# Shifts of three norms in a transformer block: minus the mean written by VectorE with one input, multiplied by the root on GpSimd behind the root

## The chip, the cores and the metric

The kernel runs on one core of one Trainium2 chip. Its time is the device time of one execution in microseconds (us), here the median of several runs. The profile is of one execution, and its span runs from the first to the last instruction.

The engines are TensorE (PE for its products, PEld for its weight loads), VectorE (DVE), ScalarE (ACT), GpSimd (POOL) and SyncE (SP), whose queue issues the DMAs. Each engine works through its own list in order and waits on semaphores for the others.

## What is computed

The input `x` has 8 x 2048 rows of 256 numbers. Everything is float32.

```python
x = L0_attn_x
xn = _layernorm(x)                     # first norm, no gain and offset
# inside s = _L0_attn_ref(xn, ...)
q, k, v = split(xn @ Wqkv + bqkv)
qp, kp = elu(q) + 1, elu(k) + 1
attn = (qp @ (kp^T v)) / (qp . sum(kp) + 1e-6)      # per batch of 2048 rows
z = layer_norm(xn + attn, g1, b1)      # second norm
ffn = (silu(z @ Wg + bg) * (z @ Wu + bu)) @ Wd + bd
s = layer_norm(z + ffn, g2, b2)        # third norm
g = silu(xn @ (ternary(weight) * scale)^T)
return x + s * g
```

A norm of a row is `row * root + shift`, with root = 1/sqrt(variance + eps) and shift = -mean * root. The change is about who computes these shifts.

## The kernel before

**Tiling.** The 16384 rows are cut into 32 groups of 512 rows (four tiles of 128), four groups to a batch. One loop over the groups is laid out as a pipeline: in the iteration that does the feed-forward net of group f, the attention of group f+1, the norm and the turned copy of group f+6 and the last norm of group f-1 are done as well. In front of it stands a filling phase, behind it two iterations that drain it. Each product is done as three products of split (high and low) parts, and the low parts are subtractions on VectorE.

**Order.** What each engine does in an iteration, and in which order, is a list written by hand: `TENSOR_JOBS`, `SCALAR_STEPS`, `VECTOR_STEPS`, `GPSIMD_STEPS`, with `FILL_...`, `END_...` and `DRAIN_...` for the ends. An engine that waits in one step holds up all steps behind it.

**The three norms.** Number k is 0 for the first norm, 1 for the one behind attention, 2 for the last. For each, VectorE takes the statistics of four tiles (`stats`, L922) and aggregates them into `mv` (`aggregate`, L929, mean and variance), and writes variance + eps into `ve` (L933). GpSimd raises it to -0.5 (`rstd`, L569). Then VectorE writes the shift from mean and root with one operation on [128, 4]: `nmr0` in `a_norm` (L978), `nmr1` in `attn_norm` (L1064), `nmr2` in `last_shift` (L1131). ScalarE applies root and shift to the rows: `x_norm` (first four groups only) and `x_res` for norm 0, `z_rows` for norm 1, `last_rows` for norm 2. From the fifth group on, `a_norm` also writes the normed rows itself (L974), from mean and root.

**Steps near the change.** On VectorE the iteration begins with `zT_low` (L1085), `k_add` (L1014) and `ffn_rows` (L1117), then `last_stats`, the four `attn` steps (L1048, L1051, L1054, L922) with `last_shift` between the first two, `h_rows` 0 (L1095), `k_max` 0 (L1021), `h_low` 0 (L1105), `h_rows` 1, `a_stats`, `h_low` 1, `q_aggregate`, `h_rows` 2, `a_norm`, `x_turn` (L985), `attn_norm`, and so on to `q_low` 1 (L1042) and `h_low` 5. On GpSimd it begins with `xn_low` 0 (L579), `last_rstd`, `last_gain` 0 (L602, waits for `last_rows` 0), `z_g1` 0 (L642), `last_offset` 0 (L608), `xn_low` 1 and `sum_k` 0 (L592, waits for `k_max` 0); later come `a_rstd` and `q_rstd`, the other row operations, `last_add` 3 (L621, releases the output's DMA and the next load of `xq` on SP's queue), and `tail_again` (L655), which waits for `h_rows` 5.

**Banks.** Products go round a ring of five PSUM banks. A job may start once the job five places before it has been read (`freed`). So product job Q 1 waits for `h_low` 1 of VectorE, the job U 0 for `attn` 0, and the job K 1 for `h_low` 3.

Of the kernel before, what the change touches and what calls it, by code (L numbers as in the profile page):

```python
# [31 lines left out]
D = 256  # L32
# [29 lines left out]
LN0 = LEAD + 1  # L62
# [21 lines left out]
def fill(text):  # L84
# [13 lines left out]
    h_high 3, x_high 1, h_high 4, silu_gate 5, xn_high 0, xn_high 1, h_high 5""")  # L98
VECTOR_STEPS = steps("""
    xk_low 0, zT_low 0, k_add 0, zT_low 1, kv_bias 0, kv_bias 1, kv_low 0, kv_low 1, ffn_rows 0,  # L100
    ffn_rows 1, k_add 1, last_stats 0, attn 0, last_shift 0, attn 1, attn 2, attn 3, h_rows 0, k_max 0,
    h_low 0, h_rows 1, a_stats 0, h_low 1, q_aggregate 0, h_rows 2, a_norm 0, x_turn 0, attn_norm 0,
    k_max 1, h_low 2, k_low 0, q_elu 0, z_turn 0, q_elu 1, q_low 0, k_low 1, h_rows 3, h_rows 4,
    q_low 1, h_low 3, x_low 0, h_rows 5, x_low 1, h_low 4, h_low 5""")
GPSIMD_STEPS = steps("""
# [10 lines left out]
    silu_gate 5, h_high 5, tail_last 0""")  # L116
END_VECTOR = steps("""
    zT_low 0, zT_low 1, ffn_rows 0, h_rows 0, ffn_rows 1, h_low 0, last_stats 0, h_rows 1, h_low 1,
    last_shift 0, h_rows 2, h_low 2, h_rows 3, h_rows 4, h_low 3, h_low 4, h_rows 5, h_low 5""")
END_GPSIMD = steps("""  # L120
    end_terms 0, z_g1 0, last_rstd 0, z_g1 1, z_g1 2, last_gain 0, last_offset 0, last_gain 1,
    last_gain 2, last_offset 1, last_gate 0, last_offset 2, last_add 0, last_gain 3, last_gate 1,
# [29 lines left out]
    k_add 3 1, a_stats 5 0, k_max 3 1, xT_low 4 0, setup_ternary 0 0, q_elu 1 0, xk_low 0 0, xT_low 4 1,  # L152
    k_add 4 0, kv_bias 0 0, kv_bias 0 1, a_norm 5 0, kv_low 0 0, kv_low 0 1, x_turn 5 0, k_max 4 0,
    k_add 4 1, attn 0 0, k_low 4 0, k_max 4 1, setup_ternary_parts 0 0, attn 0 1, attn 0 2, attn 0 3,
    q_aggregate 0 0, k_low 4 1, attn_norm 0 0, setup_d_tail 0 0, x_low 5 0, q_elu 1 1,
    setup_hidden_biases 0 0, x_low 5 1, q_low 1 0, q_low 1 1""")
FILL_GPSIMD = fill("""
    setup_masks 0 0, a_rstd 0 0, a_rstd 0 1, a_rstd 1 0, sum_k 0 0, sum_k 0 1, a_rstd 2 0, sum_k 0 2,
# [54 lines left out]
def build_kernel(nc, x, wqkv, bqkv, wg, bg, wu, bu, wd, bd, g1, b1, g2, b2, wt, out):  # L213
    f32, f32r = mybir.dt.float32, mybir.dt.float32r
    ALU, ACT = mybir.AluOpType, mybir.ActivationFunctionType
# [8 lines left out]
    with ctx:  # L224
# [3 lines left out]
        def sem(name):  # L228
# [20 lines left out]
        rstd0 = sb("rstd0", [P, LN0, TILES])  # L249
# [21 lines left out]
        nmr0 = sb("nmr0", [P, LN0, TILES])  # L271
        mv = sb("mv", [P, 3, TILES, 2])
# [8 lines left out]
        xn = sb("xn", [P, TILES, D])  # L281
        kp = sb("kp", [P, KP, 2, D])
# [10 lines left out]
        rstd1, nmr1 = norm1[:, 0, :], norm1[:, 1, :]  # L293
        rstd2, nmr2 = norm2[:, 0, :], norm2[:, 1, :]
# [32 lines left out]

        names = ("warm first_act first_warm w_bq1 w_bk w_qkh w_qkl w_abs w_sum w_scale w_half "
                 "w_vh w_vl w_neg w_tern w_ternT w_tern_r w_b1w w_row w_hb w_guh w_gul w_db w_dh w_dl w_dt "
                 "bn0 ag0 ve0 rs0 xn nm0 xh xl tn tz TX xTh xTl K k1 mK eK kp kph kpl ks XK xk xkl KV kv kvh kvl "  # L330
                 "Q mQ eQ qp qph qpl N d1 d2 xr r bn1 ag1 ve1 rs1 nm1 z TZ zTh zTl zg B sg "
                 "G GU S h hh hl ha D r2 bn2 ag2 ve2 rs2 nm2 n2 a b c o bs gs xb a_last o_last").split()
        S = {n: sem("s_" + n) for n in names}

        def parts3(hi_l, lo_l, hi_r, lo_r):

            return ((hi_l, hi_r), (lo_l, hi_r), (hi_l, lo_r))

        def job_bank(kind, g, n):
            return bank[NUMBER[kind, g, n] % RING]  # L340
# [199 lines left out]
        def _(eng):  # L540
# [140 lines left out]
            for i in ITERATIONS:  # L681
                a, q, f, last = i + LEAD, i + 1, i, i - 1
# [234 lines left out]
        def _(eng):  # L917
# [18 lines left out]
            def first_stats(p):
                pair = slice(2 * p, 2 * p + 2)
# [23 lines left out]
            def a_norm(g, p=0):  # L961
                if g == 0:
                    return first_norm(p)
                eng.wait_ge(S["rs0"], g + 2)
                if g == PLAIN:
                    eng.wait_ge(S["xn"], TILES * PLAIN)
                    eng.wait_ge(S["XK"], TILES * (g - 1))
                if g > PLAIN:
                    eng.wait_ge(S["xl"], PAIRS * (g - PLAIN))
                    eng.wait_ge(S["TX"], PAIRS * min(g, TURNED))  # L970
                if g > TURNED:
                    eng.wait_ge(S["tn"], g - TURNED)
                for t in range(TILES if g >= PLAIN else 0):
                    eng.tensor_scalar(normed(g)[:, t, :], xa[:, g % 2, t, :], mv[:, 0, t, 0:1],  # L974
                                      rstd0[:, g % LN0, t:t + 1], ALU.subtract, ALU.mult).then_inc(S["xn"], 1)
                if g >= LN0:
                    eng.wait_ge(S["xr"], TILES * (g - LN0 + 1))
                eng.scalar_tensor_tensor(out=nmr0[:, g % LN0, :], in0=mv[:, 0, :, 0], scalar=-1.0,  # L978
                                         in1=rstd0[:, g % LN0, :], op0=ALU.mult, op1=ALU.mult).then_inc(S["nm0"], 1)

            def x_turn(g, _=0):
                if g >= TURNED:
# [74 lines left out]
                eng.wait_ge(S["r"], n + 1)  # L1057
                stats(1, g, t, rz[:, g % RZ, t, :])

            def attn_norm(g, _=0):  # L1060
                eng.wait_ge(S["rs1"], g + 1)
                if g:
                    eng.wait_ge(S["z"], TILES * g)
                eng.scalar_tensor_tensor(out=nmr1, in0=mv[:, 1, :, 0], scalar=-1.0,  # L1064
                                         in1=rstd1, op0=ALU.mult, op1=ALU.mult).then_inc(S["nm1"], 1)

            def z_turn(g, _=0):
                if not ZT0 <= g < ZT1:
                    return
# [50 lines left out]
            def last_stats(g, _=0):  # L1120
# [13 lines left out]
            def end_rows(g, _=0):

# [113 lines left out]
            for i in ITERATIONS:  # L1249
# [230 lines left out]
```

## Time and profile before

| | |
|---|---|
| median of 3 runs | 1210.86 us (1210.26 to 1211.26) |
| profiled execution: its time | 1212.66 us |
| profiled execution: span | 1211.0 us |
| TensorE products busy | 1190.9 us, 98% |
| VectorE busy | 1082.2 us, 89% |
| ScalarE busy | 953.3 us, 79% |
| GpSimd busy | 841.7 us, 70% |
| granted TensorE clock | 0.998 of full speed |

The profiled execution took 1.66 us more than its span, which lies ahead of the first and behind the last instruction, and 1.8 us more than the median of the runs. Busy time of TensorE is modelled, since products are pipelined; whether it really waits is read from the distances between the starts of its products.

### The profile page before, as it was taken

The page shows a single profiled execution, that of the slowest core. Times are in us where ns is not written, and L with a number is a line of the kernel's source. Part 1 is how long each engine was busy: PE and PEld are TensorE (multiplying, and loading weights), DVE is VectorE, ACT ScalarE, POOL GpSimd, SP SyncE. Part 2 cuts the span into 40 slices and gives each one's busy share as a digit, 9 for nine tenths or more (in the row PEclk, how much of TensorE's full clock was granted, in tenths as well). Part 3 has the DMA queues.
Part 4 walks back from the last instruction along what each step waited for, and adds up shares of the span by engine and source line. Part 5 has one row for each costly group of instructions (what it writes and reads, how often), then busy time and mean ns, then how long its engine had stood idle before and what let it go on. Part 6 is the DMA issues. An engine that isn't in the chain of part 4 may idle for free.

```text
span 1211.0 us, 24021 instructions
## 1 busy us (share of the span) xinstructions
PE 1190.9 (98%) x7550; PEld 1070.2 (88%) x7550; DVE 1082.2 (89%) x2467; ACT 953.3 (79%) x1557; POOL 841.7 (70%) x994
## 2 busy tenths in 40 slices
PE   8999999999999999999999999999999999999997
PEld 6889998989988999989999988999988899888886
DVE  6988999999999999999999999999999999777765
ACT  7787888878888887888878888778797788867753
POOL 3443787767787776787767777667776677766676
PEclk9999999999999999999999999999999999999999
DMA  7213432334432334432234432234332343222201
GB/s 217 74 50 88 123 106 70 88 105 123 123 104 72 87 106 123 118 103 78 87 106 122 121 104 74 74 120 123 108 96 63 101 123 105 70 71 61 76 22 35
DMA packets 137524, 115.61 MB, mean 95 GB/s; under 512 B 12340, under 2 KB 122294, under 8 KB 137399
## 3 DMA queue, kind: packets, MB, share of 16 engines
q1 hardware_dynamic: 137398, 114.08, 32.2%
q8 instruction: 62, 1.02, 0.3%
q14 instruction: 64, 0.52, 0.1%
HBM read 67.38 MB, written 46.67 MB: 94 GB/s over the span
## 4 chain that ended last, share of the span: by engine, by line
PE 86%; DVE 7%; issue 2%; ACT 2%; DMA 1%; POOL 1%; SPq 0%; DVEq 0%; POOLq 0%; ACTq 0%
PE bank L1271 61%; PE d_bank L1271 17%; PE xk_bank L1271 7%; DVE st L922 1%; DMA z_turned<-xa 1%; DMA xa<-z_turned 1%; DVE rz L1054 1%; PE bank L1285 1%; DVE bank L1095 0%; DVE h_l L1105 0%; ACT rz L695 0%; DVE zT_l L1085 0%; POOL norm L569 0%; ACT hs L695 0%; DVE kp L1014 0%
## 5 line engine op out<-in xcount | busy, mean ns | idle before, releaser
L1271 PE MATMUL bank<-zT_h,wgu_h 128*128 128x512 f32 x704 | 275.6, 391 | 1.1 <-DVE rz L1054 1.0
L1271 PE MATMUL bank<-zT_l,wgu_h 128*128 128x512 f32 x704 | 275.7, 392 | 0.0
L1271 PE MATMUL bank<-zT_h,wgu_l 128*128 128x512 f32 x704 | 275.4, 391 | 0.0
L695 ACT ACTIVATE rz<-rz,norm 128x256 f32<-128x256 f32 x252 | 140.5, 596 | 57.7 <-DVE norm L1131 57.1
L569 POOL TENSOR_TENSOR norm<-ve,consts 128x4 f32<-128x4 f32 x64 | 72.9, 1139 | 153.6 <-DVE ve L933 153.5
L1271 PE MATMUL d_bank<-wd_h,h_h 128*128 128x256 f32 x640 | 179.2, 280 | 0.1
L1271 PE MATMUL d_bank<-wd_h,h_l 128*128 128x256 f32 x640 | 179.0, 280 | 0.0
L1271 PE MATMUL d_bank<-wd_l,h_h 128*128 128x256 f32 x640 | 179.0, 280 | 0.0
L1095 DVE SCALAR_TENSOR_TENSOR bank<-bank,hb,hs 128x512 f32<-128x512 f32 x160 | 117.9, 754 | 54.0 <-ACT hs L695 42.3
L695 ACT ACTIVATE h_h<-bank 128x512 fp32r<-128x512 f32 x160 | 95.8, 599 | 80.9 <-DVE bank L1095 80.5
L1271 PEld LDWEIGHTS bank<-zT_l,wgu_h 128*128 128x128 f32 x704 | 132.1, 188 | 28.8
L1271 PEld LDWEIGHTS bank<-zT_h,wgu_h 128*128 128x128 f32 x704 | 132.7, 189 | 25.8 <-DVE rz L1054 3.3
L695 ACT ACT_TABLE_LOAD x116 | 148.8, 1283 | 4.1 <-POOL wd_l L678 1.2
L1271 PEld LDWEIGHTS bank<-zT_h,wgu_l 128*128 128x128 f32 x704 | 132.2, 188 | 20.6
L695 ACT ACTIVATE hs<-bank,hb 128x512 f32<-128x512 f32 x192 | 128.3, 685 | 15.0 <-PE bank L1271 13.6
L592 POOL TENSOR_TENSOR ksum<-ksum,kp 128x256 f32<-128x256 f32 x120 | 106.9, 891 | 46.7 <-DVE kp L1021 43.3
L1105 DVE TENSOR_TENSOR h_l<-bank,h_h 128x512 fp32r<-128x512 f32 x160 | 110.0, 688 | 23.1 <-ACT h_h L695 17.4
L1271 PEld LDWEIGHTS d_bank<-wd_h,h_h 128*128 128x128 f32 x640 | 120.2, 188 | 3.1 <-DVE h_l L1105 0.5
L1271 PEld LDWEIGHTS d_bank<-wd_h,h_l 128*128 128x128 f32 x640 | 120.2, 188 | 2.7
L1271 PEld LDWEIGHTS d_bank<-wd_l,h_h 128*128 128x128 f32 x640 | 122.0, 191 | 0.0
L642 POOL TENSOR_TENSOR rz<-rz,g1b 128x256 f32<-128x256 f32 x128 | 118.0, 932 | 0.0
L602 POOL TENSOR_TENSOR rz<-rz,g2b 128x256 f32<-128x256 f32 x124 | 90.4, 739 | 35.0 <-ACT rz L695 35.0
(163 smaller groups left out, 3576.3 us busy)
## 6 DMA issues: line engine op xcount, KB each, us to landing
xq<-in_L_attn_x_dram SPq DMA_DIRECT2D x32, 512.0 KB, 6.0
xa<-in_L_attn_x_dram SPq DMA_DIRECT2D x31, 512.0 KB, 3.9
out_dram<-rz SPq DMA_DIRECT2D x31, 512.0 KB, 5.0
z_turned<-xa SPq DMA_DIRECT2D x120, 128.0 KB, 3.3
xa<-z_turned SPq DMA_DIRECT2D x30, 512.0 KB, 4.1
turned<-xa SPq DMA_DIRECT2D x108, 128.0 KB, 2.5
xa<-turned SPq DMA_DIRECT2D x27, 512.0 KB, 3.9
rz<-in_L_attn_Wg_dram SPq DMA_DIRECT2D x1, 640.0 KB, 5.2
```

The lines of the kernel that those rows point to most:

```text
L569: eng.tensor_tensor(dst, ve[:, k, :], neg_half[:, 0:1].to_broadcast([P, TILES]), ALU.pow).then_inc(S[f"rs{k}"], 1)
L592: eng.tensor_tensor(ksum[:, slot, :], ksum[:, slot, :], part, ALU.add).then_inc(S["ks"], 1)
L602: eng.tensor_tensor(row_, row_, g2b[:, :], ALU.mult).then_inc(S["a"], 1)
L642: eng.tensor_tensor(row_, row_, g1b[:, :], ALU.mult).then_inc(S["zg"], 1)
L695: return eng.activation(out_, in_, func, **kw).then_inc(S[name], 1)
L922: eng.bn_stats(st[:, k, t, :], rows).then_inc(S[f"bn{k}"], 1)
L1054: eng.scalar_tensor_tensor(out=rz[:, g % RZ, t, :], in0=num[:, 0:D], scalar=den[:, n % 2, 1:2], in1=rz[:, g % RZ, t, :], op0=ALU.mult, op1 ...
L1095: eng.scalar_tensor_tensor(out=hidden(g, c)[0:rows, :], in0=up, scalar=hb[0:rows, HC + c:HC + c + 1], in1=hs[0:rows, n % 2, :], op0=ALU.ad ...
L1105: eng.tensor_tensor(h_l[:, slot, :], hidden(g, c)[:, :], h_h[:, slot, :].bitcast(f32), ALU.subtract).then_inc(S["hl"], 1)
L1271: ins = eng.matmul(dst, left, right, start=first and n == 0, stop=last and n == len(pairs) - 1, **kw)
L1285: ins = eng.transpose(dst[:, c * D + t * P:c * D + (t + 1) * P], src[:, 2 * p + t, c * P:(c + 1) * P], ident[:, :])
```

## The change

The shift is now made in two parts. VectorE writes minus the mean into the place of the shift, straight behind `ve`, with an operation that has one input. GpSimd, straight behind the root, waits for both and multiplies that place by the root. The steps `attn_norm` and `last_shift` and the operation at the end of `a_norm` are gone from VectorE. New semaphores `ng0` to `ng2` count the minus means; `nm0` to `nm2` still count finished shifts, now signalled by GpSimd. The very first group keeps its own path (`first_stats`, `first_norm`). The last group of norm 2 needs no shift: VectorE still writes minus its mean, GpSimd leaves the multiply out.

```diff
 VECTOR_STEPS
-    ... last_stats 0, attn 0, last_shift 0, attn 1, ...
+    ... last_stats 0, attn 0, attn 1, ...
-    ... a_norm 0, x_turn 0, attn_norm 0, k_max 1, ...
+    ... a_norm 0, x_turn 0, k_max 1, ...
...
+        def shift_of(k, g):
+            return nmr0[:, g % LN0, :] if k == 0 else nmr1 if k == 1 else nmr2
...
 def rstd(k, g, dst):            # GpSimd
                 eng.tensor_tensor(dst, ve[:, k, :], neg_half[:, 0:1].to_broadcast([P, TILES]),
                                   ALU.pow).then_inc(S[f"rs{k}"], 1)
+                if k == 2 and g == GROUPS - 1:
+                    return
+                eng.wait_ge(S[f"rs{k}"], g + 1 + (k == 0))
+                eng.wait_ge(S[f"ng{k}"], g + (k > 0))
+                to = shift_of(k, g)
+                eng.tensor_tensor(to, to, dst, ALU.mult).then_inc(S[f"nm{k}"], 1)
...
 def aggregate(k, g):            # VectorE
-                    if g and t == 0:
-                        eng.wait_ge(S[f"nm{k}"], g + (k == 0))
+                    if g > (k == 0) and t == 0:
+                        eng.wait_ge(S[f"ng{k}"], g - (k == 0))
+                    if g == 1 and k == 0 and t == 0:
+                        eng.wait_ge(S["nm0"], 2)
...
                 eng.tensor_scalar(ve[:, k, :], mv[:, k, :, 1], LN_EPS, None, ALU.add)\
                    .then_inc(S[f"ve{k}"], 1)
+                if k == 0 and g >= LN0:
+                    eng.wait_ge(S["xr"], TILES * (g - LN0 + 1))
+                if k == 1 and g:
+                    eng.wait_ge(S["z"], TILES * g)
+                if k == 2 and g:
+                    eng.wait_ge(S["n2"], TILES * min(g, GROUPS - 1))
+                eng.tensor_scalar(shift_of(k, g), mv[:, k, :, 0], -1.0, None, ALU.mult).then_inc(S[f"ng{k}"], 1)
...
 def a_norm(g, p=0):             # VectorE
-                if g >= LN0:
-                    eng.wait_ge(S["xr"], TILES * (g - LN0 + 1))
-                eng.scalar_tensor_tensor(out=nmr0[:, g % LN0, :], in0=mv[:, 0, :, 0], scalar=-1.0,
-                                         in1=rstd0[:, g % LN0, :], op0=ALU.mult, op1=ALU.mult).then_inc(S["nm0"], 1)
...
-            def attn_norm(g, _=0):
-                eng.wait_ge(S["rs1"], g + 1)
-                if g:
-                    eng.wait_ge(S["z"], TILES * g)
-                eng.scalar_tensor_tensor(out=nmr1, in0=mv[:, 1, :, 0], scalar=-1.0,
-                                         in1=rstd1, op0=ALU.mult, op1=ALU.mult).then_inc(S["nm1"], 1)
...
-            def last_shift(g, _=0):
-                if g < GROUPS - 1:
-                    eng.wait_ge(S["rs2"], g + 1)
-                    if g:
-                        eng.wait_ge(S["n2"], TILES * g)
-                    eng.scalar_tensor_tensor(out=nmr2[:, :], in0=mv[:, 2, :, 0], scalar=-1.0,
-                                             in1=rstd2[:, :], op0=ALU.mult, op1=ALU.mult).then_inc(S["nm2"], 1)
```

## Rows read from the trace of the kernel before

**Rows 1.** The page, its part on busy time by engine.

```profile
PE 1190.9 (98%) x7550; PEld 1070.2 (88%) x7550; DVE 1082.2 (89%) x2467; ACT 953.3 (79%) x1557; POOL 841.7 (70%) x994
```

**Rows 2.** Timeline of TensorE: first product of N 0 in seven groups.

```profile
74.96 0.29 PE L1271 MATMUL bank<-kv_h,qp_h 128*128 128x258 f32 x1
...
548.31 0.28 PE L1271 MATMUL bank<-kv_h,qp_h 128*128 128x258 f32 x1
...
584.09 0.28 PE L1271 MATMUL bank<-kv_h,qp_h 128*128 128x258 f32 x1
...
694.09 0.28 PE L1271 MATMUL bank<-kv_h,qp_h 128*128 128x258 f32 x1
...
730.01 0.28 PE L1271 MATMUL bank<-kv_h,qp_h 128*128 128x258 f32 x1
...
768.01 0.35 PE L1271 MATMUL bank<-kv_h,qp_h 128*128 128x258 f32 x1
...
1022.88 0.28 PE L1271 MATMUL bank<-kv_h,qp_h 128*128 128x258 f32 x1
```

**Rows 3.** Waits of TensorE's loads from 110 to 1150 us: total, times, longest.

```profile
PEld bank L1271 <- DVE h_l L1105: 4.1, 13, 0.4
```

**Rows 4.** Timeline of TensorE: first load of Q 1 in the group of 658.01.

```profile
671.56 0.19 PEld L1271 LDWEIGHTS bank<-xT_h,wq_h 128*128 128x128 f32 x1 [0.37 <-DVE h_l L1105]
```

**Rows 5.** Timeline of one group, VectorE and TensorE's Q 1: start, length, operation.

```profile
552.46 0.14 DVE L1131 SCALAR_TENSOR_TENSOR norm<-mv,norm 128x4 f32<-128x4 f32 x1
552.52 0.15 DVE L1048 TENSOR_SCALAR den<-bank 128x1 f32<-128x1 f32 x1
...
556.90 0.68 DVE L1021 TENSOR_TENSOR kp<-kp,ku 128x512 f32<-128x512 f32 x1
...
560.68 0.17 DVE L933 TENSOR_SCALAR ve<-mv 128x4 f32<-128x4 f32 x1
560.76 0.69 DVE L1105 TENSOR_TENSOR h_l<-bank,h_h 128x512 fp32r<-128x512 f32 x1
...
561.75 0.39 PE L1271 MATMUL bank<-xT_h,wq_h 128*128 128x512 f32 x1
```

**Rows 6.** One line's instructions: count, length in ns least/median/greatest, first and last start.

```profile
L933 DVE TENSOR_SCALAR ve<-mv x95: 170/170/732, 11.7 to 1205.0; 128x4 f32<-128x4 f32 x95
...
L978 DVE SCALAR_TENSOR_TENSOR nmr<-mv,rstd x31: 150/725/731, 13.0 to 1002.6; 128x4 f32<-128x4 f32 x31
...
L569 POOL TENSOR_TENSOR norm<-ve,consts x64: 1017/1018/1389, 67.6 to 1205.2; 128x4 f32<-128x4 f32 x64
```

**Rows 7.** Groups of instructions by shape, VectorE and GpSimd: busy us, mean ns.

```profile
L1064 DVE SCALAR_TENSOR_TENSOR norm<-mv,norm 128x4 f32<-128x4 f32 x32 | 11.3, 355 | 1.3 <-POOL norm L569 1.3
...
L630 POOL TENSOR_TENSOR sg<-sg,g2b 128x1024 f32<-128x1024 f32 x1 | 2.4, 2397 | 0.1
```

**Rows 8.** Timeline of the group of 548.31, GpSimd and ScalarE, with idle time and releaser.

```profile
551.38 1.02 POOL L569 TENSOR_TENSOR norm<-ve,consts 128x4 f32<-128x4 f32 x1 [4.22 <-DVE ve L933]
...
552.64 0.60 ACT L695 ACTIVATE rz<-rz,norm 128x256 f32<-128x256 f32 x1 [1.64 <-DVE norm L1131]
...
553.31 0.73 POOL L602 TENSOR_TENSOR rz<-rz,g2b 128x256 f32<-128x256 f32 x1 [0.92 <-ACT rz L695]
...
555.40 1.28 POOL L579 TENSOR_TENSOR xn_l<-xn,xn_h 128x512 fp32r<-128x512 f32 x1
...
578.27 1.00 POOL L655 CAST ht<-hs 32x512 fp32r<-32x512 f32 x1 [1.55 <-DVE hs L1095]
579.50 0.60 POOL L655 CAST ht<-hs 32x512 fp32r<-32x512 f32 x1 [0.22 <-POOL ht L655]
```

**Rows 9.** Timeline of VectorE around `q_low` 1 in two groups.

```profile
574.08 1.42 DVE L1095 SCALAR_TENSOR_TENSOR bank<-bank,hb,hs 128x512 f32<-128x512 f32 x2 [1.19 <-ACT hs L695]
575.41 0.72 DVE L1042 TENSOR_TENSOR qp_l<-qp,qp_h 128x512 fp32r<-128x512 f32 x1
...
721.18 1.29 DVE L1042 TENSOR_TENSOR qp_l<-qp,qp_h 128x512 fp32r<-128x512 f32 x1
```

More of the change, by code:

```diff
@@ L100 @@
     xk_low 0, zT_low 0, k_add 0, zT_low 1, kv_bias 0, kv_bias 1, kv_low 0, kv_low 1, ffn_rows 0,
-    ffn_rows 1, k_add 1, last_stats 0, attn 0, last_shift 0, attn 1, attn 2, attn 3, h_rows 0, k_max 0,
-    h_low 0, h_rows 1, a_stats 0, h_low 1, q_aggregate 0, h_rows 2, a_norm 0, x_turn 0, attn_norm 0,
+    ffn_rows 1, k_add 1, last_stats 0, attn 0, attn 1, attn 2, attn 3, h_rows 0, k_max 0,
+    h_low 0, h_rows 1, a_stats 0, h_low 1, q_aggregate 0, h_rows 2, a_norm 0, x_turn 0,
     k_max 1, h_low 2, k_low 0, q_elu 0, z_turn 0, q_elu 1, q_low 0, k_low 1, h_rows 3, h_rows 4,
@@ L118 @@
     zT_low 0, zT_low 1, ffn_rows 0, h_rows 0, ffn_rows 1, h_low 0, last_stats 0, h_rows 1, h_low 1,
-    last_shift 0, h_rows 2, h_low 2, h_rows 3, h_rows 4, h_low 3, h_low 4, h_rows 5, h_low 5""")
+    h_rows 2, h_low 2, h_rows 3, h_rows 4, h_low 3, h_low 4, h_rows 5, h_low 5""")
 END_GPSIMD = steps("""
@@ L154 @@
     k_add 4 1, attn 0 0, k_low 4 0, k_max 4 1, setup_ternary_parts 0 0, attn 0 1, attn 0 2, attn 0 3,
-    q_aggregate 0 0, k_low 4 1, attn_norm 0 0, setup_d_tail 0 0, x_low 5 0, q_elu 1 1,
+    q_aggregate 0 0, k_low 4 1, setup_d_tail 0 0, x_low 5 0, q_elu 1 1,
     setup_hidden_biases 0 0, x_low 5 1, q_low 1 0, q_low 1 1""")
@@ L329, in build_kernel @@
                  "w_vh w_vl w_neg w_tern w_ternT w_tern_r w_b1w w_row w_hb w_guh w_gul w_db w_dh w_dl w_dt "
-                 "bn0 ag0 ve0 rs0 xn nm0 xh xl tn tz TX xTh xTl K k1 mK eK kp kph kpl ks XK xk xkl KV kv kvh kvl "
-                 "Q mQ eQ qp qph qpl N d1 d2 xr r bn1 ag1 ve1 rs1 nm1 z TZ zTh zTl zg B sg "
-                 "G GU S h hh hl ha D r2 bn2 ag2 ve2 rs2 nm2 n2 a b c o bs gs xb a_last o_last").split()
+                 "bn0 ag0 ve0 rs0 ng0 xn nm0 xh xl tn tz TX xTh xTl K k1 mK eK kp kph kpl ks XK xk xkl KV kv kvh kvl "
+                 "Q mQ eQ qp qph qpl N d1 d2 xr r bn1 ag1 ve1 rs1 ng1 nm1 z TZ zTh zTl zg B sg "
+                 "G GU S h hh hl ha D r2 bn2 ag2 ve2 rs2 ng2 nm2 n2 a b c o bs gs xb a_last o_last").split()
         S = {n: sem("s_" + n) for n in names}
@@ L1261, in _ @@
                     "q_aggregate": (q, lambda g, _: aggregate(1, g)), "last_stats": (last, last_stats),
-                    "attn_norm": (q, attn_norm), "z_turn": (q, z_turn), "last_shift": (last, last_shift),
+                    "z_turn": (q, z_turn),
                     "end_rows": (last, end_rows), "xT_low": (a + 1, xT_low)})
```

## The prediction

> **What bounds the kernel now.** I read the page first: TensorE is busy 98% of the span, VectorE 89%, GpSimd 70% [rows 1]. Since busy time of TensorE is modelled, I then took the starts of one product, the first of N 0, in each group from the timeline. An undisturbed group takes 584.09 - 548.31 = 35.78 us [rows 2], and no group takes less; a group that also does the KV products takes 37.76 us at least (584.09 to 621.85). From 74.96 to 1022.88 there are 20 groups of the first kind and 6 of the second: 20 x 35.78 + 6 x 37.76 = 942.16 us, against 947.92 us in the trace. So TensorE loses 5.8 us in this whole stretch, and nothing that VectorE, ScalarE or GpSimd save can give more than that there.
>
> Where are they lost? In TensorE's waits the longest steady entry is for `h_low`, 13 times [rows 3]. Each is at the same place: the first load of Q 1, whose bank was read by `h_low` 1 [rows 4]. I measured the slack there in all groups. In the undisturbed group `h_low` 1 ends at 560.76 + 0.69 = 561.45 and Q 1 starts at 561.75 without a wait: 0.30 us [rows 5]. In the 13 late groups the distance is 0.05 to 0.06 us, which is what the handover takes. So 14 groups have 0.25 us to spare, 13 have nothing: whatever is put on VectorE ahead of `h_low` 1 reaches TensorE in those.
>
> Why are some late? Partly by the port of GpSimd: at `q_low` 1 VectorE and GpSimd arrive together; usually it takes 0.72 us, in the group of 694.09 1.29 us [rows 9]. That group took 35.92 us, and the next, a KV group, 38.00 us [rows 2]: 0.14 + 0.24 = 0.38 us for one lost race. It was lost in 5 groups.
>
> **The change, part by part.**
>
> *VectorE, removed.* 31 x 0.63 (`nmr0`, mostly 0.725 us, once it waits behind GpSimd) + 32 x 0.355 (`nmr1`) + 31 x 0.16 us (`nmr2`, read as the other two) = 36 us busy [rows 6, 7]. Added: 95 operations like the one that writes `ve`, 0.17 us each, 16 us [rows 6]. In a group VectorE saves about 0.7 us. But 0.32 and 0.73 of what is removed lie between `h_rows` 2 and `k_max` 1, and behind them VectorE waits 1.19 us for ScalarE ahead of `h_rows` 3 [rows 9]. ScalarE gets no earlier: from `h_high` 1 to there it works without a break. The saving goes into that wait. I cost it at nothing; if VectorE did not wait there, it would be worth up to the 5.8 us.
>
> *VectorE, ahead of `h_low` 1.* From one `ve` write to the next operation 0.08 us pass (560.68 to 560.76) [rows 5]; I take this for each added write. Ahead of `h_low` 1 there are two, in `last_stats` and in `a_stats`: +0.16. What goes away is `last_shift`, which took 552.52 - 552.46 = 0.06 us [rows 5]. Net +0.10 us. The waits in front of the new writes (`xr`, `z`, `n2`, the own `ng`) are for steps of the iteration before. 13 groups x 0.10 = 1.3 us; in the 14 others it comes out of the 0.25.
>
> *How long can the new write be?* Its twin has a median of 170 ns and once took 732 [rows 6], when a GpSimd operation had started just ahead of it. At the `a_stats` write GpSimd has nothing to do but wait for `ve`, so I take 0.17, and keep 0.56 more as the upper end.
>
> The Trainium skill (SBUF — State Buffer, Who interferes with whom) states that VectorE and GpSimd share a pair of ports as an exclusive lock, taken by a VectorE instruction with two SBUF inputs or in a two-port mode, which `tensor_scalar` can enter. The trace agrees for two inputs: `nmr0` takes 150 ns alone and 725 beside GpSimd [rows 6]. By this rule the one-input write is not safe either, and a wait of 0.56 us at each would give the time of the port rival below.
>
> *GpSimd, added.* 94 multiplies on [128, 4] with a wait for the own root. No row shows one. The nearest multiplies are 0.73 us for 256 columns and 2.40 for 1024 [rows 7, 8]: 2.17 ns a column, so 0.18 us fixed and 0.19 us for 4 columns, my value. Bounds: 0.15 us, what `nmr0` takes alone on VectorE, and 1.02, the root on the same tile [rows 6]. The wait for its own result costs at most the 0.22 us between the two copies of `tail_again` [rows 8]; I take 0.1.
>
> The Trainium skill (GPSIMD Engine Reference, Key points) puts elementwise work on VectorE at about twice the speed of GpSimd. By that the multiply would be 0.30 us instead of 0.19, which speaks against the move but stays under the limit worked out next.
>
> *Norm 2, the first of the three.* Today the root ends at 552.40, `last_shift` at 552.60, `last_rows` 0 starts at 552.64 [rows 5, 8]. Now: 552.40 + 0.1 + 0.19 = 552.69, some 0.1 us later. ScalarE idled 1.64 us there [rows 8], and `h_rows` 0 needs what follows only later: hidden. GpSimd's row operations slip with it; `xn_low` 1 ends at 556.68, `k_max` 0, which has two SBUF inputs, starts at 556.90 [rows 5, 8]. With 0.15 us of slack behind `k_max` (`h_low` 0 waits for ScalarE), a slip of some 0.35 us is free. That is a multiply with its wait of 0.55 us; beyond it VectorE is held.
>
> *Norms 0 and 1.* Both multiplies stand in a stretch in which GpSimd works without a break and then waits 1.55 us for `h_rows` 5 [rows 8]. Two times 0.29 = 0.6 us, about one row operation (0.70), come out of that. `z_rows` comes behind `q_exp` 0 on ScalarE and is not waiting for its shift today. `last_add` 3 moves later by 0.6 to 1.2 us, and with it the output DMA and the load of `xq` on SP; `x_res` then starts as much later, and it has the 1.64 us of ScalarE's idle ahead of `last_rows` 0 as cover. If that were gone, `k_exp` and `silu_gate` 0 would follow late.
>
> *Filling and draining.* The shift of the second group is waited for at 13 us, where ScalarE and then TensorE follow directly: +0.1. Norm 2's write stands ahead of `attn` 0 in the iteration near 1120 where TensorE waits for it, +0.08, and ahead of `end_rows` at the very end, +0.08. The stall of VectorE for `nmr1` in the filling goes, but there ScalarE's `z_rows` sets TensorE's next turn: nothing.
>
> Sum: 1.3 + 0.26 = 1.6 us. The profiled execution's 1212.66 us would be 1214.2, its span 1212.6; that execution stood 1.8 us over the median, so the median goes from 1210.86 to about 1212.4.
>
> **Rivals.**
>
> *Everything is absorbed.* The new writes slip in where VectorE waited anyway, or races fall slightly better: 1210.9 to 1211.2. For it: 1.3 us is small. Against: the handover of 0.05 us in 13 groups.
>
> *The race at `q_low` 1.* GpSimd arrives there one operation later than now. As each collision sets its phase anew by VectorE's ends, I expect the same meeting with another operation. If it falls badly in all 27 groups instead of 5, 22 x 0.38 = 8.4 us more: 1220.8. It decides once GpSimd starts an operation there ahead of VectorE.
>
> *The multiply costs like the root.* 0.1 + 1.02 us moves `xn_low` 1 by 0.92, `k_max` 0 by 0.68 and `h_low` 0 by 0.53. With the 0.10, 13 groups lose 0.63 and 14 lose 0.38: 13.5 us, 1224.6. Against: most of the root's microsecond should be the power.
>
> *The port.* The write in `a_stats` waits 0.56 us each time: 13 x 0.66 + 14 x 0.41 = 14.3 us, 1225.4. Against: 94 of 95 twins didn't.
>
> *Faster.* VectorE reaches `z_turn` some 0.3 us earlier and GpSimd misses `q_low` 1, so that the lateness handed from group to group breaks up. If half of the 5.8 us goes, 1210.86 - 2.9 + 0.3 = 1208.3; all of it, 1205.4. For it: late groups come in rows behind lost races and KV groups. Against: VectorE's 1.19 us of waiting stands between the saving and `q_low` 1. It decides if the race is never lost.
>
> **How the numbers follow.** The forecast gets 0.48 (own range 1211.3 to 1213.8), absorbed 0.14, the race 0.14, the multiply 0.06, the port 0.03, faster 0.15. A difference under 0.2%, 2.4 us, can't be told from none here, so the borders are 1208.4 and 1213.3. Faster: 0.13 of the last. Same: 0.36 of the forecast, 0.14, and 0.02 of faster. Slower: 0.12 of the forecast and 0.14 + 0.06 + 0.03. Faster 0.13, same 0.52, slower 0.35. The range reaches down to the faster case's half, and up into the race in most groups: 1208.6 to 1218.
>
> **What would show it.** `h_low` 1 ends 0.10 us later behind the start of N 0, and Q 1 starts later by that in the late groups; the new writes take 0.17 us, the multiply about 0.2 and starts 0.1 behind the root; GpSimd's wait in front of `tail_again` shrinks from 1.55 to about 0.9; VectorE's wait ahead of `h_rows` 3 grows; undisturbed groups still take 35.78 us. It is wrong if the multiply is over 0.45 us, or if `q_low` 1 takes 1.29 us in more or fewer than a handful of groups.

## The result

| | before | after |
|---|---|---|
| median | 1210.56 us (1210.0 to 1211.26) | 1216.35 us (1216.18 to 1217.8) |
| profiled execution: span | 1211.0 us | 1214.5 us |
| first N 0 of the steady stage | 74.96 | 74.57 |
| the 27 groups from there | 984.3 us | 988.2 us |

The change makes the kernel 5.8 us slower, a ratio of 1.005 (95% interval 1.0038 to 1.0062). The forecast was 1212.4 in a range of 1208.6 to 1218.0: the time lies in the range, but "within 0.2%" was the likeliest case and it is slower, by three and a half times the 1.6 us of the sum. The profiled execution of the kernel before took 1212.66 us, 2.1 us more than its median, that of the changed kernel 1216.24 us, about its median. So the two profiles show 3.5 us of the 5.8.

The page, busy time by engine, is to be read beside [rows 1]. The prediction took 36 us off VectorE and added 16, so it should be some 20 us less busy; it is 1.5 us less, since it now waits longer inside other operations. GpSimd gains 94 small instructions.

```profile
PE 1192.6 (98%) x7550; PEld 1066.9 (88%) x7550; DVE 1080.7 (89%) x2468; ACT 953.1 (78%) x1557; POOL 860.5 (71%) x1088
```

The rhythm of TensorE, the same product as in [rows 2]:

```profile
74.57 0.29 PE L1270 MATMUL bank<-kv_h,qp_h 128*128 128x258 f32 x1
...
110.36 0.28 PE L1270 MATMUL bank<-kv_h,qp_h 128*128 128x258 f32 x1
...
549.90 0.28 PE L1270 MATMUL bank<-kv_h,qp_h 128*128 128x258 f32 x1
...
586.06 0.28 PE L1270 MATMUL bank<-kv_h,qp_h 128*128 128x258 f32 x1
```

The filling ends 0.4 us earlier than before, and the 27 groups take 3.9 us more: 2.0 of them in the six KV groups, 1.9 in the others. The first two groups take 35.79 and 35.78 us. No other group does: ordinary groups take 36.01 to 36.48, the KV groups 38.23 to 38.36 (before 37.76 to 38.37). This group takes 586.06 - 549.90 = 36.16. TensorE's loads show three places, where [rows 3] had 4.1 us in 13 waits; from 110 to 1030 us:

```profile
PEld bank L1270 <- DVE h_l L1112: 8.0, 24, 0.7
PEld bank L1270 <- DVE rz L1068: 4.8, 23, 0.3
PEld bank L1270 <- issue: 2.6, 6, 0.5
```

The first is `h_low` 1 ahead of Q 1, now in 24 groups. The second is `attn` 0 ahead of U 0, which had a slack of 0.5 us in the undisturbed groups before (1.8 us in 8 waits in the same stretch). The third stands in the six KV groups, ahead of their N 0; the profile names no releaser for it, and it was 1.1 us in 4 waits before. These waits are more than what TensorE loses, 15.4 us against 10.3 us of lost time: a load of a running TensorE starts 0.22 us ahead of its product (561.53 and 561.75 for Q 1 in the undisturbed group), and its wait costs nothing up to there.

Now one group, VectorE on the way to `h_low` 1 and then around the two `q_low` (to be read beside [rows 5, 9]):

```profile
562.69 0.17 DVE L944 TENSOR_SCALAR ve<-mv 128x4 f32<-128x4 f32 x1
562.77 0.16 DVE L952 TENSOR_SCALAR nmr<-mv 128x4 f32<-128x4 f32 x1
562.84 0.68 DVE L1112 TENSOR_TENSOR h_l<-bank,h_h 128x512 fp32r<-128x512 f32 x1
...
572.93 1.19 DVE L1056 TENSOR_TENSOR qp_l<-qp,qp_h 128x512 fp32r<-128x512 f32 x1 [0.29 <-ACT qp_h L704]
574.04 1.23 DVE L1044 TENSOR_TENSOR kp_l<-kp,kp_h 128x512 fp32r<-128x512 f32 x1
...
576.10 1.42 DVE L1102 SCALAR_TENSOR_TENSOR bank<-bank,hb,hs 128x512 f32<-128x512 f32 x2 [0.83 <-ACT hs L704]
577.42 1.08 DVE L1056 TENSOR_TENSOR qp_l<-qp,qp_h 128x512 fp32r<-128x512 f32 x1
```

The new write costs 562.84 - 562.77 = 0.07 us ahead of `h_low` 1, as forecast. What was not forecast is the last row: `q_low` 1 takes 1.08 us, 0.36 more than the 0.72 of [rows 9]. It took over 0.9 us in 6 of these 27 groups before and does so in 25 now. GpSimd beside it:

```profile
562.94 1.02 POOL L572 TENSOR_TENSOR rstd<-ve,consts 128x4 f32<-128x4 f32 x1 [0.31 <-DVE ve L944]
564.04 0.20 POOL L579 TENSOR_TENSOR nmr<-nmr,rstd 128x4 f32<-128x4 f32 x1
564.19 0.75 POOL L617 TENSOR_TENSOR rz<-rz,b2b 128x256 f32<-128x256 f32 x1
564.89 1.21 POOL L572 TENSOR_TENSOR norm<-ve,consts 128x4 f32<-128x4 f32 x1
566.18 0.20 POOL L579 TENSOR_TENSOR norm<-norm 128x4 f32<-128x4 f32 x1
566.33 0.74 POOL L624 TENSOR_TENSOR rz<-rz,sg 128x256 f32<-128x256 f32 x1
...
572.84 0.73 POOL L617 TENSOR_TENSOR rz<-rz,b2b 128x256 f32<-128x256 f32 x1
573.64 1.08 POOL L624 TENSOR_TENSOR rz<-rz,sg 128x256 f32<-128x256 f32 x1
...
577.22 0.74 POOL L630 TENSOR_TENSOR rz<-rz,xq 128x256 f32<-128x256 f32 x1
577.93 1.19 POOL L601 TENSOR_TENSOR ksum<-ksum,kp 128x256 f32<-128x256 f32 x1
```

A multiply takes 0.20 us and starts 0.08 behind the root; from root to the next operation 564.19 - 562.94 = 1.25 us pass, 0.26 more than before. Further down the reader sees the meetings. `last_offset` 3 starts at 572.84, `q_low` 0 at 572.93, and `q_low` 0 waits for nearly all of it (1.19). `last_add` 3 starts at 577.22, `q_low` 1 at 577.42, and waits again. The lateness then travels by VectorE's order, in medians of the ordinary groups from the third on: `h_low` 3 starts 0.30 us later behind N 0 than before, `zT_low` 0 0.27 us later, and `h_low` 1 of the next group ends 0.07 us later.

### The profile page after: what moved, and what is told of

It is laid out like the page before. It is cut to its first block, busy times and chain, and to the rows that moved or that the text cites. A ratio compares the mean times of both kernels' runs of the same rounds, so it can differ in the third digit from the quotient of the medians.

```text
span 1214.5 us, 24152 instructions
## 1 busy us (share of the span) xinstructions
PE 1192.6 (98%) x7550; PEld 1066.9 (88%) x7550; DVE 1080.7 (89%) x2468; ACT 953.1 (78%) x1557; POOL 860.5 (71%) x1088
## 4 chain that ended last, share of the span: by engine, by line
DVE 32%; PE 29%; ACT 21%; issue 15%; DMA 1%; POOL 1%; ACTq 0%; DVEq 0%; SPq 0%; POOLq 0%
PE bank L1270 20%; PE d_bank L1270 6%; ACT rz L704 5%; DVE st L931 5%; DVE bank L1102 5%; DVE rz L1068 4%; DVE h_l L1112 3%; PE xk_bank L1270 3%; ACT hs L704 2%; ACT L704 2%; ACT h_h L704 2%; DVE xT_l L1005 2%; ACT qp L704 2%; ACT ku L704 2%; ACT kp_h L704 2%
## 5 line engine op out<-in xcount | busy, mean ns | idle before, releaser
L601 POOL TENSOR_TENSOR ksum<-ksum,kp 128x256 f32<-128x256 f32 x120 | 109.9, 916 | 42.4 <-DVE kp L1035 38.9
L1112 DVE TENSOR_TENSOR h_l<-bank,h_h 128x512 fp32r<-128x512 f32 x160 | 110.0, 687 | 31.8 <-ACT h_h L704 28.7
L611 POOL TENSOR_TENSOR rz<-rz,g2b 128x256 f32<-128x256 f32 x124 | 101.7, 832 | 27.6 <-ACT rz L704 27.6
L624 POOL TENSOR_TENSOR rz<-rz,sg 128x256 f32<-128x256 f32 x124 | 109.5, 883 | 5.0
```

Source lines behind the costliest of these rows:

```text
L601: eng.tensor_tensor(ksum[:, slot, :], ksum[:, slot, :], part, ALU.add).then_inc(S["ks"], 1)
L611: eng.tensor_tensor(row_, row_, g2b[:, :], ALU.mult).then_inc(S["a"], 1)
L624: eng.tensor_tensor(row_, row_, sg[:, g % SG, t, :], ALU.mult).then_inc(S["c"], 1)
L1112: eng.tensor_tensor(h_l[:, slot, :], hidden(g, c)[:, :], h_h[:, slot, :].bitcast(f32), ALU.subtract).then_inc(S["hl"], 1)
```

## The experiments

The experiments share one figure, read from the timelines: over the 27 groups from the first steady one on, how long `q_low` 1 takes on average and in how many groups over 0.9 us. "Excess" is what these groups take together over 35.78 us (37.76 for the six KV groups), in the profiled execution, which can lie some us off the median: 2.1 above it in the kernel before, 5.8 in quiet_before. The kernels ran in four rounds, each with runs of the kernel before beside it, so kernels of different rounds are compared by their ratios.

| kernel | median us | ratio to before (95%) | `q_low` 1 mean us, over 0.9 in | excess us |
|---|---|---|---|---|
| before | 1210.56 | | 0.834, 6 | 6.4 |
| after | 1216.35 | 1.005 (1.0038 to 1.0062) | 1.054, 25 | 10.3 |
| writes_only | 1222.64 | 1.011 (1.0095 to 1.0124) | 1.050, 17 | 16.2 |
| multiplies_only | 1218.34 | 1.0073 (1.0059 to 1.0086) | 1.129, 24 | 12.8 |
| late_writes | 1215.23 | 1.0043 (1.0031 to 1.0056) | 1.056, 25 | 8.5 |
| one_more | 1219.73 | 1.0079 (1.0066 to 1.0093) | 1.130, 20 | 13.1 |
| yield_after | 1212.16 | 1.0011 (1.0003 to 1.002) | 0.680, 0 | 6.0 |
| yield_before | 1213.90 | 1.0025 (1.0016 to 1.0034) | 0.708, 0 | 9.1 |
| yield_late | 1209.83 | 0.9998 (0.9989 to 1.0006) | 0.680, 0 | 5.0 |
| yield_writes | 1218.93 | 1.0063 (1.0049 to 1.0076) | 0.680, 0 | 13.5 |
| norm2_alone | 1210.56 | 0.9999 (0.999 to 1.0007) | 0.788, 3 | 4.9 |
| quiet_before | 1242.43 | 1.0271 (1.0245 to 1.0297) | 0.680, 0 | 42.1 |
| quiet_after | 1240.89 | 1.0251 (1.0237 to 1.0264) | 0.680, 0 | 31.8 |
| quiet_late | 1243.14 | 1.0267 (1.0254 to 1.0281) | 0.680, 0 | 36.9 |

### One half of the change at a time

The writes alone, into a tile that nobody reads, in the kernel before:

```diff
+                    if g > (k == 0) and t == 0:
+                        eng.wait_ge(S[f"ng{k}"], g - (k == 0))
...
                 eng.tensor_scalar(ve[:, k, :], mv[:, k, :, 1], LN_EPS, None, ALU.add)\
                    .then_inc(S[f"ve{k}"], 1)
+                eng.tensor_scalar(spare[k], mv[:, k, :, 0], -1.0, None, ALU.mult).then_inc(S[f"ng{k}"], 1)
```

> The kernel before with the three new VectorE writes alone: each norm's negated mean goes to a spare tile that nobody reads, the old shifts stay on VectorE and GpSimd's queue is unchanged. Writes theory (the operations put ahead of h_low 1 are the 5.8 us): about 1216, q_low 1 as short as before. GpSimd theory (its later arrival at the two q_low is the 5.8 us): 1210.5 to 1211.5. Sum theory (a group loses what writes and races come to together, less the 0.25 us of slack that 14 groups had): the writes alone, 0.16 us in the 13 groups without slack, give 1 to 2.5 us, 1211.5 to 1213, with the undisturbed groups still at 35.78.

The multiplies alone, also into a spare tile:

```diff
                                   ALU.pow).then_inc(S[f"rs{k}"], 1)
...
+                eng.wait_ge(S[f"rs{k}"], g + 1 + (k == 0))
...
+                eng.tensor_tensor(spare[k], ve[:, k, :], dst, ALU.mult).then_inc(S[f"ng{k}"], 1)
```

> The kernel before with the three small GpSimd multiplies alone: each writes variance term times root to a spare tile that nobody reads, directly behind the root and with the wait for it; VectorE is unchanged, old shifts included. Writes theory: no change, 1210.5 to 1211. GpSimd theory: the whole 5.8 us, about 1216, with q_low 1 at about 1.08 us in every group. Sum theory: q_low 1 at about 1.08 in every group too, but a group loses 0.38 less 0.25 = 0.13 us, 27 x 0.13 = 3.5: about 1214.

Measured: 1222.64 and 1218.34 us. Each half costs more than the whole, 12.4 and 8.1 us (from the before of those runs, 1210.23) against 5.8. Writes and multiplies alone can't be added up to that. Both halves keep the old shifts on VectorE, so what their removal gives back is a part of the difference that they don't show. All three theories had the writes alone too low, the sum theory by 10 us. `q_low` 1 in the multiplies is as two of them said, lost in 24 groups; the price of it was over twice the 3.5 us of the sum theory.

The trace of the writes alone has a second cause. Its group from 551.38:

```profile
566.17 1.87 DVE L978 TENSOR_SCALAR xn<-xa,mv,rstd 128x256 f32<-128x256 f32 x4
567.97 0.70 DVE L982 SCALAR_TENSOR_TENSOR nmr<-mv,rstd 128x4 f32<-128x4 f32 x1
568.59 1.23 DVE L989 STREAM_TRANSPOSE xa<-xn 128x1024 f32<-128x1024 f32 x1
...
573.72 0.38 SPq L435 DMA_DIRECT2D xa<-turned  x1
574.19 2.20 SPq L445 DMA_DIRECT2D z_turned<-xa  x4
579.15 0.38 SPq L449 DMA_DIRECT2D xa<-z_turned  x1
...
583.05 1.16 ACT L696 ACTIVATE zT_h<-xa 128x512 fp32r<-128x512 f32 x2
```

And the same steps of the kernel before, in the group from 548.31:

```profile
562.51 1.38 DVE L974 TENSOR_SCALAR xn<-xa,mv,rstd 128x256 f32<-128x256 f32 x4
563.80 0.73 DVE L978 SCALAR_TENSOR_TENSOR nmr<-mv,rstd 128x4 f32<-128x4 f32 x1
564.45 1.23 DVE L985 STREAM_TRANSPOSE xa<-xn 128x1024 f32<-128x1024 f32 x1
...
569.58 0.38 SPq L434 DMA_DIRECT2D xa<-turned  x1
570.33 2.10 SPq L444 DMA_DIRECT2D z_turned<-xa  x4
575.08 0.38 SPq L448 DMA_DIRECT2D xa<-z_turned  x1
...
579.15 1.16 ACT L695 ACTIVATE zT_h<-xa 128x512 fp32r<-128x512 f32 x2
```

Counted from the start of the group, `x_turn` starts at 17.21 instead of 16.14, the load of the turned z is issued at 27.77 instead of 26.77 and `zT_high` starts at 31.67 instead of 30.84. The medians over the ordinary groups say the same: 17.21 against 16.47, 27.82 against 27.06, 32.00 against 31.26. Ahead of `zT_high` ScalarE waits for this load in 22 groups of the writes alone, 15.7 us together, and in 12 of the kernel before, 5.2 us. The load stands on SP behind the round trip of the turned x, so a late `x_turn` makes ScalarE's and VectorE's parts of z late too. In the changed kernel `x_turn` starts at 16.10 (median), 0.37 us earlier than before, because the shift of norm 0 no longer stands ahead of it. The writes alone do not have that; they keep the shift, it takes 0.70 us, and `xn` ahead of it is drawn out. The multiplies alone keep the shift too, but it happens to take 0.15 us there and `x_turn` starts at 16.18; theirs is the longer wait at `q_low` 1, 1.129 us on average against 1.054 in the changed kernel.

### The two writes off the way

The changed kernel with the write of norm 0 behind `h_low` 1 and that of norm 2 between denominator and reciprocal of `attn` 0:

```diff
-    h_low 0, h_rows 1, a_stats 0, h_low 1, q_aggregate 0, ...
+    h_low 0, h_rows 1, a_stats 0, h_low 1, a_negated 0, q_aggregate 0, ...
...
                    .then_inc(S["d1"], 1)
+                if t == 0 and g >= 2 and is_late(2, g - 2):
+                    negated(2, g - 2)
                 eng.wait_ge(S["d1"], n + 1)
```

> The changed kernel with two of the three writes moved in the steady groups: the negated mean of norm 0 is written behind h_low 1 and not ahead of it, that of norm 2 inside attn 0 between the denominator and its reciprocal, where VectorE waits for itself. GpSimd's operations are unchanged. Writes theory: back to about 1211. GpSimd theory: 1216, as the changed kernel. Sum theory: 0.15 to 0.2 us less ahead of h_low 1 in all 27 groups, 4 to 5 us: 1211.5 to 1212.5, with q_low 1 still at 1.08.

Measured 1215.23, a ratio of 1.0043 whose interval overlaps that of the changed kernel. `q_low` 1 stays as it was (over 0.9 us in 25 groups). So the only term that I had priced in the steady stage is worth about 1 us at most, which the intervals can't tell from nothing, and the writes theory falls. The sum theory expected 4 to 5 us and falls too.

### One more small multiply

```diff
                 eng.tensor_tensor(to, to, dst, ALU.mult).then_inc(S[f"nm{k}"], 1)
+                for n in range(1 if k == 1 else 0):
+                    ...
+                    eng.tensor_tensor(spare[n % 3], dst, dst, ALU.mult).then_inc(S["ex"], 1)
```

> The changed kernel with one more small GpSimd multiply, to a spare tile, behind that of norm 1: GpSimd reaches q_low 0 some 0.15 us later still. Writes theory: same as the changed kernel, 1216.3. GpSimd and sum theories: the meeting is a matter of phase, not of load: q_low 0 at 23.03 now starts 0.09 us behind a GpSimd operation and waits for it; 0.15 us more and VectorE is first (0.69 us instead of 1.19). Then q_low 1 meets another phase; if it too is first, the kernel gets faster by 3 to 5 us, 1211 to 1213, although work was added; if it is not, it stays within 1 us of 1216.

Measured 1219.73. The first half came true: `q_low` 0 now starts ahead of GpSimd's operation and takes 0.69 us (median) instead of 1.19. The second didn't: `q_low` 1 starts so that it meets the next one at its very beginning, 1.29 us (median). That the first meeting is won by adding work shows that phase decides it and not load; where the second would fall I could not say. My "within 1 us of 1216" missed by 2.7.

### GpSimd gives way at q_low 1

The changed kernel, `last_add` 3 held until `q_low` 1 is done; the same in the kernel with late writes; in the kernel before and in the writes alone it is `sum_k` 2 that is held:

```diff
                     eng.wait_ge(S["c"], TILES * g + t + 1)
+                    if t == TILES - 1 and g < GROUPS - 3:
+                        eng.wait_ge(S["qpl"], DC * (g + 4))
```

> The changed kernel, in which GpSimd holds its last_add 3 back until q_low 1 is done; GpSimd has 1.45 us to spare ahead of tail_again and the held operations take 1.45. Race theory (the changed kernel's loss is q_low 1 waiting for a GpSimd operation in every group, and the writes ahead of h_low 1 count only for what is beyond the slack): q_low 1 takes 0.68 to 0.73 us in all groups, h_low 1 ends at about 13.25 after N 0, most groups return to 35.78; 27 x 0.35 us of lateness are gone, of which the 10.25 us that its groups now take over the undisturbed ones are the most that can come back: 1207 to 1210, faster than both kernels. Writes theory: no more than 1 us of gain, 1215 to 1216.5. Hold theory (the held operations run into tail_again or x_low and hand the time back): 1214 to 1217 with x_low over 0.9 us.

> The kernel before, in which GpSimd holds its sum_k 2 back until q_low 1 is done. Race theory: the 6 lost races are gone, most of the groups that follow them return to 35.78: 1205.5 to 1208. Rival: the late groups there have another cause (the KV products), then no more than 2 us: 1208.5 to 1210.

> The changed kernel with both: last_add 3 held back until q_low 1 is done, and the two writes behind h_low 1 and inside attn 0. Race theory: with the race gone, 0.1 us ahead of h_low 1 comes out of the slack, so that moving the writes is worth 0 to 1.5 us over the hold alone: 1206 to 1209. Writes theory: 1214 to 1215, as with the writes moved alone.

> The kernel before with the three new VectorE writes to a spare tile (1222.6 us, 12.4 over before), now with sum_k 2 on GpSimd held back until q_low 1 is done. Race theory: the 12.4 us were not the writes but the q_low 1 that they moved behind the start of a GpSimd operation (1.28 us in 17 groups): 1208 to 1211. Direct theory (VectorE's own added work is what costs): 1218 to 1222.

Measured: 1212.16, 1213.90, 1209.83 and 1218.93. In the changed kernel the hold takes the ratio from 1.005 to 1.0011, about 0.39% or 4.7 us (3.9 us by the medians, each less the before of its runs); the intervals are apart. That is the largest part of the loss, gained back by one wait that adds nothing to VectorE. It was to give 1207 to 1210 and gave less, and in the kernel before the hold costs 3 to 4 us where I expected a gain. One pair of traces says why, here the changed kernel with the hold, VectorE and then GpSimd:

```profile
576.77 0.68 DVE L1058 TENSOR_TENSOR qp_l<-qp,qp_h 128x512 fp32r<-128x512 f32 x1
577.37 0.68 DVE L1114 TENSOR_TENSOR h_l<-bank,h_h 128x512 fp32r<-128x512 f32 x1
577.97 0.91 DVE L1007 TENSOR_TENSOR xT_l<-xa,xT_h 128x512 fp32r<-128x512 f32 x1
...
577.59 0.73 POOL L632 TENSOR_TENSOR rz<-rz,xq 128x256 f32<-128x256 f32 x1 [0.98 <-DVE qp_l L1058]
578.29 1.19 POOL L601 TENSOR_TENSOR ksum<-ksum,kp 128x256 f32<-128x256 f32 x1
```

`q_low` 1 is at 0.68, but the held operation now runs from 577.59 and `x_low` 0, which starts at 577.97, takes 0.91 instead of 0.68. So 0.40 us are won here and 0.23 handed back; `x_low` 0 is drawn out like this in 25 of the 27 groups. The kernel before has little to win (6 groups) and pays 0.26 in most of them: `x_low` 0 takes 0.94 us (median). My text for it looked at `q_low` 1 alone, the mistake of the prediction once more.

With the hold, moving the two writes is worth 2.3 us (1212.16 to 1209.83; the runs, 1211.6 to 1212.54 and 1209.3 to 1211.36, do not overlap), more than the 0 to 1.5 expected. With both, nothing is left of the loss: the ratio to the kernel before is 0.9998 (0.9989 to 1.0006). In the writes alone the hold takes the ratio from 1.011 to 1.0063, 5.7 us (3.7 by the medians). There the late `x_turn` and the 0.16 us ahead of `h_low` 1 remain and are the likely rest; neither was taken away by itself, so this is not shown.

### Norm 2 alone

```diff
+MOVED = (2,)
...
+                if k not in MOVED or (k == 2 and g == GROUPS - 1):
+                    return
+                eng.wait_ge(S[f"rs{k}"], g + 1 + (k == 0))
```

> Only the shift of norm 2 is moved (write in last_stats, multiply behind its root), those of norms 0 and 1 stay as before. GpSimd waits for ScalarE right behind that multiply, so its operations meet VectorE's q_low 0 and q_low 1 in the phase of before. Meeting theory: q_low 1 is lost in as few groups as before, 1210 to 1212. If it is lost in most groups (over 15), it is VectorE's own 0.02 to 0.08 us that moves the phase, and the time is 1213 to 1218.

Measured 1210.56, ratio 0.9999 (0.999 to 1.0007): no change, `q_low` 1 over 0.9 us in 3 groups. GpSimd has a wait for ScalarE behind this multiply, which swallows it. So norm 2 by itself costs nothing, and the loss needs norms 0 and 1, whose multiplies stand in the stretch in which GpSimd works without a break. Norms 0 and 1 without norm 2 were not run.

### GpSimd kept away from the whole chain

Three edits of GpSimd's order: `last_add` 3 waits for `x_low` 0, `sum_k` 2 goes behind `tail_again`, and `sum_k` 2 waits for both `zT_low`.

```diff
-    z_g1 3, sum_k 1, last_add 3, sum_k 2, tail_again 0, tail_again 1, sum_k 3""")
+    z_g1 3, sum_k 1, last_add 3, tail_again 0, tail_again 1, sum_k 2, sum_k 3""")
...
+                    if t == 2 and g >= LEAD:
+                        eng.wait_ge(S["zTl"], DC * (g - LEAD + 2))
```

> The kernel before with GpSimd kept away from the four two-input VectorE operations of the chain that leads to h_low 1: last_add 3 waits until x_low 0 is done, sum_k 2 goes behind tail_again, and sum_k 2, sum_k 3 and xn_low 0 wait until zT_low 1 is done, in a stretch in which GpSimd waits 5.24 us today. Meeting theory (what a small edit gains or loses is how much these four VectorE operations wait for GpSimd, beyond 0.25 us of slack): q_low 1 0.70, x_low 0 0.68, zT_low 0 and 1 0.68 instead of 0.73 to 1.29, 0.68, 1.11 and 1.18; VectorE is 0.9 to 1.3 us earlier at h_low 1, no group waits there, all are at 35.78 and the KV groups at 37.76: 1204 to 1206. Rival: the held GpSimd operations come too late for k_add 1 or for the root of norm 2, and TensorE waits there: 1209 to 1216.

> The changed kernel with the same three edits of GpSimd's order. Meeting theory: the change is then free, since its 0.1 us ahead of h_low 1 comes out of a slack of about 1 us: within 1 us of the kernel before with the same edits, 1204 to 1206.5. Direct theory (the writes and multiplies cost by themselves): 4 to 6 us over it, as without the edits.

> The changed kernel with its two writes moved off the way to h_low 1 and the same three edits of GpSimd's order. Meeting theory: the same as the changed kernel with the edits, within 0.5 us, because what stands ahead of h_low 1 no longer decides. Direct theory: 1 to 2 us faster than that one.

Measured 1242.43, 1240.89 and 1243.14: 30 us slower, so the rival case, and worse than it. The four operations did what they should: `q_low` 1, `x_low` 0 and both `zT_low` take 0.68 to 0.69 us. But the held `last_add` 3 now meets `x_low` 1, which takes 1.17 us in 18 groups of the kernel before with the edits and in 6 of the changed one. And the held sums come too late. TensorE's and VectorE's waits in the kernel before with these edits:

```profile
PE bank L1275 <- POOL ksum L594: 21.0, 7, 3.1
...
DVE kp L1018 <- POOL ksum L594: 11.5, 20, 1.0
```

The KV products need the batch's whole sum, and `k_add` 1 needs the place that `sum_k` 3 frees. Of the excess, 32.9 us are in the six KV groups, and waiting is only a part of it. In the first of them TensorE waits 3.08 us for the sum and starts again at 183.84; from 182.69 to 189.52 the granted clock in the rows is 0.50, which is the 1.2 GHz level, and the products on 256 columns start every 0.21 us instead of 0.12. Five of the six KV groups have such a stretch, 27.3 us together, and TensorE works for 24.6 us of them. At half the clock that is an estimated 12 us lost, beside some 18 us of waiting. The kernel before has no such stretch from the filling to 1206 us.

The 20 ordinary groups other than the last have 4.9 us of excess in the kernel before and 4.3 in the changed one (4.4 and 6.2 without the edits). So the 1.8 us that the change cost them do not show here. But that is one profile each, and `x_low` 1 is drawn out more often in the first of the two, so it is a hint and no proof. The times of the three kernels (1.0271, 1.0251, 1.0267, with overlapping intervals) can't be told apart.

## Why the prediction was right and where it was wrong

**The view was right.** Q 1 waits for `h_low` 1, undisturbed groups have 0.25 us to spare, and VectorE's saving between `h_rows` 2 and `k_max` 1 doesn't reach `q_low` 1: it starts 27.4 us behind N 0 in both kernels (medians). The place was wrong, though. The wait ahead of `h_rows` 3 was to grow and shrank, from 1.19 to 0.83 us. The saving is used up ahead of it: `k_max` 1 takes 1.06 us instead of 0.68 beside GpSimd, and VectorE waits for ScalarE 0.36 us ahead of `h_low` 2 and 0.29 ahead of `q_low` 0, where it waited 0.13 and not at all (medians). No wait for `x_res` or the output's DMA took its place, as said. GpSimd's wait ahead of `tail_again`, which was to shrink to about 0.9 us, is 1.45 (median), 0.07 less than before.

**The new operations were priced right.** The write costs 0.07 to 0.08 us ahead of `h_low` 1, its length is 0.155 to 0.172 us in all 95, and the multiply's 0.19 was 0.20 with 0.08 ahead of it. No write waited for GpSimd, so the port rival did not happen. It was not put to the test either: when a write starts, GpSimd has at most 0.06 us left of an operation. The one `ve` write of this kernel that starts 0.04 us behind a row operation of GpSimd, [128, 256], takes 0.72 us.

**The removal touches more than the sum looked at.** "I cost it at nothing" left out the round trip of x: `x_turn` comes 0.37 us earlier, and the load of z behind it on SP's queue at 26.71 after N 0 instead of 27.06 (medians). ScalarE's waits for this load ahead of `zT_high` fall from 5.2 us in 12 groups to 0.2 us in 2. Yet `zT_high` starts at 31.23 against 31.26, so in these traces no time comes of it. The writes alone, where `x_turn` and the load come later than before, are the slowest of the kernels without a reordered GpSimd. What the removal is worth by itself was not measured.

**The step that failed** is the term of the sum: 0.10 us in 13 groups and nothing else in the steady stage. It rests on the sentence in the race rival, "As each collision sets its phase anew by VectorE's ends, I expect the same meeting with another operation". The phase is not set anew in full. Of the 2 x 0.26 us that GpSimd comes later, about 0.4 arrive at `q_low` 0: `last_offset` 3 starts at 22.84 after N 0 instead of 22.45 (medians), while VectorE arrives at 22.94 in both. So VectorE meets the start of an operation and not its middle. From there GpSimd stands 3.6 us behind `q_low` 0's start at `sum_k` 1 instead of 3.2, and `q_low` 1 runs into `last_add` 3. It was the rival with 14% that happened, and the sign of being wrong that the prediction named, a long `q_low` 1 in more than a handful of groups. The range holds the measured time because its upper border was drawn up into this rival, not because the sum was right. Its price was 22 x 0.38 = 8.4 us; measured are 19 more groups and an average of 0.22 us more (1.054 - 0.834), 5.9 us of waiting in 27 groups, and 3.9 to 4.7 us of the kernel's time come back when the meeting is taken away.

**The slack was counted once.** With 0.36 us in nearly every group the 0.25 us are used up by the meeting, and then the two writes can count in all groups: 24 waits at Q 1 and 23 at U 0, where the prediction had 13 and, in the steady stage, none. In full they would be 27 x 2 x 0.07 = 3.8 us; moving them gave back about 1, so most of this is not borne out. Only two groups still take 35.78 us. The prediction had 14 left undisturbed; of these, five took 35.77 or 35.78 us before, and two KV groups 37.76.

What stays open: why moving the writes wins 1 us or less without the hold and 2.3 with it, what stands ahead of N 0 in the KV groups, and how the 12.4 us of the writes alone divide.

## What to carry to other kernels

Where two engines share something that lets one in at a time, an added 0.2 us on the engine that is not the bottleneck is not costed by its length, but by where in the other's operation each later meeting falls: list every such meeting up to the next real wait, write down how far apart the two arrive, and move one by the added time. Where a wait followed the added time (norm 2 here) it cost nothing; in the stretch without a wait the later meetings shifted. A hold that clears one meeting makes the next one, so look at the two-input operations behind it as well, and at who needs what is held. Where TensorE comes to wait for it, look at the granted clock too.

## What was unexpected of the hardware

A VectorE operation with one tensor input can be drawn out too: the four `xn` operations on [128, 256] took 1.38 us together in the kernel before and 1.87 in the writes alone, with these operations on GpSimd beside them:

```profile
566.16 1.10 POOL L570 TENSOR_TENSOR norm<-ve,consts 128x4 f32<-128x4 f32 x1
567.15 0.74 POOL L616 TENSOR_TENSOR rz<-rz,sg 128x256 f32<-128x256 f32 x1
```

The three `xn` that start beside the root, from 566.17 on, take 0.41 us each, the median of this line. It is the fourth, started with GpSimd's multiply at 567.14, that takes 0.91. So it is in 25 groups of that run. Beside the root small writes were not drawn out either: in the late writes 26 of them start with some 0.6 us of the root still to run and take 0.16 us. But the one `ve` that starts behind a row operation takes 0.72. So in these runs it is the row operations of GpSimd that hold up one-input operations of VectorE and not the root on [128, 4]. Why, and whether it is size or kind, was not tried.

The cost of a meeting at `q_low` is a matter of tenths of a microsecond: 0.83 us when it starts some 0.5 us behind GpSimd's operation, 1.19 at 0.1 us behind, 1.29 when both start together, and 0.69 when it is first. There is one rule in these numbers: in the kernels before and after, each of the 79 `q_low` from 75 us on that started beside a running GpSimd operation and took over 0.78 us ended 0.54 to 0.56 us behind the end of that operation, wherever it had started.
